# A macaron block on one core: two width tests with branches, TensorE kept busy ahead of the first products, and another order in the opening

## The reference

```python
x = x + 0.5 * ffn(layernorm(x))
x = x + attn(layernorm(x))
x = x + 0.5 * ffn(layernorm(x))
# ffn(x):  h = norm(x) * gamma + beta;  w1 = (fc1_q - 128) * fc1_scales per group of 128 rows
#          y = silu(h @ w1 + fc1_bias);  z = y @ w2 + fc2_bias;  returns x + 0.5 * z
# attn(x): a = sigmoid(x@Wa+ba); b = x@Wb+bb; c = tanh(x@Wc+bc)
#          s = a*s + (1-a)*b over time;  returns (c*s)@Wy + by + x@Wd + bd
```

## Time and profile before

| | |
|---|---|
| median of three runs | 689.95 us |
| the profiled execution | 690.4 us, span 687.6 us, granted clock 0.999 |
| TensorE busy | 668.0 us, 97%, 3224 matmuls |
| ScalarE, VectorE, GpSimd busy | 653.4 (95%), 634.8 (92%), 604.8 us (88%) |
| chain that ended last | TensorE 90%, ScalarE 3%, VectorE 3% |

### The profile page before, as it was taken

One profiled execution on the slowest core, in us unless ns is written; L12 is line 12 of the kernel. 1 busy time (PEld: TensorE's weight loads), 2 busy tenths in 40 slices (PEclk: granted clock), 3 DMA queues, 4 the chain that ended last, 5 costly groups with the idle time before them and its releaser, 6 DMA issues.

```text
span 687.6 us, 13669 instructions
## 1 busy us (share of the span) xinstructions
PE 668.0 (97%) x3224; PEld 539.2 (78%) x3224; DVE 634.8 (92%) x1329; ACT 653.4 (95%) x1095; POOL 604.8 (88%) x673
## 2 busy tenths in 40 slices
PE   3999999999999999999999999999999999999997
PEld 3678888888888878778877887788888888888885
DVE  5789999999999999889999998899999999999987
ACT  4899999999999999889999999999999999999994
POOL 4899999999999999857766789999999999999973
PEclk9999999999999999999999999999999999999999
DMA  8670000000000000000000000000000000000001
GB/s 254 172 236 4 1 0 0 0 0 0 0 0 0 1 0 2 1 1 1 0 0 0 0 1 1 30 33 32 31 31 31 31 31 31 31 31 32 32 32 63
DMA packets 19962, 20.22 MB, mean 29 GB/s; under 512 B 1564, under 2 KB 19666, under 8 KB 19922
## 3 DMA queue, kind: packets, MB, share of 16 engines
q1 hardware_dynamic: 19824, 19.74, 9.3%
q10 hardware_dynamic: 98, 0.02, 0.0%
HBM read 11.37 MB, written 8.39 MB: 29 GB/s over the span
## 4 chain that ended last, share of the span: by engine, by line
PE 90%; ACT 3%; DVE 3%; issue 2%; DMA 1%; ACTq 0%; POOL 0%; DVEq 0%; POOLq 0%
PE ps_z L1009 38%; PE ps_fc L1009 33%; PE ps_fc L1142 8%; PE ps_tr L1002 5%; PE ps_tr L1070 4%; PE ps_fc L1150 2%; PE ps_z L1002 1%; DMA rows<-in_L_attn_bc 1%; DVE z_acc L762 1%; ACT ps_fc L576 1%; ACT g_hi L593 1%; DVE stats L699 1%; ACT g_full L591 0%; DVE resid L887 0%; ACTq L530 0%
## 5 line engine op out<-in xcount | busy, mean ns | idle before, releaser
L410 POOL TENSOR_TENSOR g_lo<-g_full,g_hi 128x512 fp32r<-128x512 f32 x256 | 332.9, 1300 | 24.7 <-ACT g_hi L593 21.8
L762 DVE SCALAR_TENSOR_TENSOR z_acc<-ps_z,cols,z_acc 128x512 f32<-128x512 f32 (+1 forms) x449 | 322.2, 742 | 24.2 <-PE ps_z L1009 16.4
L1009 PE MATMUL ps_fc<-h_hi,q_sb 128*128 128x512 f32 x512 | 213.4, 417 | 1.4 <-ACT ps_fc L576 1.4
L1009 PE MATMUL ps_z<-g_hi,q_sb 128*128 128x512 f32 x512 | 202.4, 395 | 0.1
L1009 PE MATMUL ps_fc<-h_lo,q_sb 128*128 128x512 f32 x512 | 202.3, 395 | 0.0
L1009 PE MATMUL ps_z<-g_lo,q_sb 128*128 128x512 f32 x512 | 200.6, 392 | 0.0
L591 ACT ACTIVATE g_full<-ps_fc,safe_scale 128x512 f32<-128x512 f32 x256 | 194.8, 761 | 3.9 <-PE ps_fc L1009 2.2
L593 ACT ACTIVATE g_hi<-ps_fc,safe_scale 128x512 fp32r<-128x512 f32 x256 | 196.2, 766 | 0.0
L576 ACT ACTIVATE ps_fc<-ps_fc,bias,ratio 128x512 f32<-128x512 f32 x193 | 157.9, 819 | 1.8 <-DVE bias L873 1.8
L1009 PEld LDWEIGHTS ps_z<-g_hi,q_sb 128*128 128x128 f32 x512 | 96.1, 188 | 25.0 <-DVE z_acc L762 2.7
L1009 PEld LDWEIGHTS ps_fc<-h_hi,q_sb 128*128 128x128 f32 x512 | 97.3, 190 | 21.0 <-ACT ps_fc L576 2.1
(11 more groups left out here) (110 smaller groups left out, 820.4 us busy)
## 6 DMA issues: line engine op xcount, KB each, us to landing
resid<-in_L_attn_x SPq DMA_DIRECT2D x15, 512.0 KB, 4.6
out_x<-resid SPq DMA_DIRECT2D x15, 512.0 KB, 2.9
q_int<-in_L_ffn_fc_q SPq DMA_DIRECT2D x4, 512.0 KB, 7.3
resid<-in_L_attn_x SPq DMA_DIRECT2D x2, 256.0 KB, 3.0
out_x<-resid SPq DMA_DIRECT2D x2, 256.0 KB, 2.7
wd_sb<-in_L_attn_Wd SPq DMA_DIRECT2D x1, 256.0 KB
wy_raw<-in_L_attn_Wy SPq DMA_DIRECT2D x2, 64.0 KB
bias_rows<-in_L_attn_by SPq DMA_DIRECT2D x1, 128.0 KB
```

Of the source, the lines that this page charges most:

```text
L410: nc.gpsimd.tensor_tensor(g_lo[:, g % 4, :], g_full[:, g % 4, :], g_hi[:, g % 4, :].bitcast(F32), ALU.subtract).then_inc(g_ready, 1)
L762: nc.vector.scalar_tensor_tensor(out=z, in0=bank_of(g, n, par)[:, tokens], scalar=col(R_S2 + KC * g + n), in1=z, op0=ALU.mult, op1=ALU.add ...
L1009: last = nc.tensor.matmul(out, w, v, start=start and i == 0, stop=stop and i == len(pairs) - 1, skip_group_check=not start)
```

## The change

1. TensorE issues 18 matmuls of 128x512 on a matrix of ones (`keep_busy`) before the rows' transpose, 2 and 3 more around the bias products. Their output is overwritten.
2. The width test is done twice: once for q1 (its two parts joined), once for all. TensorE branches on the first before the opening groups f0 to f3 (`opening`), and on the second before the rest. VectorE has one conditional block as before, now behind the second test, with a nested one for the wide q1 bias.
3. q2's first half is converted on GpSimd, its second on ScalarE. The rows' transpose goes to another bank, and ScalarE copies the columns after its half of xhat and after q1's first chunk. The turns don't wait for the columns.
4. VectorE: ratio, lower_h c0, bias fold and lower_h c1 stand ahead of statistics(1), which stands ahead of the last maximum, the second test and VectorE's half of xhat for tile 1. That half was behind variance(2). `join_largest`, `find_width` and `prepare_wide` take a number for the test and are otherwise what they were.
5. In tile 0: tile 1's rsqrt behind g_low0 and its xhat behind g_low1 on GpSimd, residual at f4 and f5 (was f2 and f3), turns at f5 and f7 (was 3 and 5), lower_h at 6 and 7 (was 4 and 6).

```diff
         halves = (range(0, SUB // 2), range(SUB // 2, SUB))
+        FIRST_TURN_AT, FIRST_LOWER_AT = (5, 7), (6, 7)
+        FIRST_RESIDUAL_AT = {4: (0, 1), 5: (2, 3)}
+        def first_or(ff0, before, first, usual):
+            return first if ff0 == 0 and not before else usual[before]
         q2_halves = (slice(0, FC // 2), slice(FC // 2, FC))
...
                     ff, ln = t + ff0, t + ln0
-                    residual_at, normalise_at = RESIDUAL_AT[before], NORMALISE_AT[before]
+                    residual_at, normalise_at = first_or(ff0, before, FIRST_RESIDUAL_AT, RESIDUAL_AT), NORMALISE_AT[before]
                     for f in range(FC):
...
                             g_low(ff - 1, FC - 1, 1 - par)
-                        elif ff0 == 0:
+                        if ff0 == 0 and not before and f == 1:
                             rsqrt(ln0 + 1, 1, True)
-                        if ff0 == 0 and not before and f == 1:
+                        if ff0 == 0 and not before and f == 2:
                             normalise(ln0 + 1, 1, 1, halves[0], True)
...
                     prepare_columns()
+                    pool.wait_ge(q2_loaded[0], 16)
+                    nc.gpsimd.tensor_scalar(q2_sb[:, q2_halves[0], :], q2_int[:, q2_halves[0], :], -ZERO_POINT, None,
+                                            ALU.add).then_inc(q2_ready[0], 1)
                     residual(ln0, 0, 1)
...
                     convert_q1(0)
+                    act.wait_ge(rows_turned, 1)
+                    nc.scalar.activation(cols[:, :], ps_fc1[:, 3, 0:ROWS], ACT.Copy).then_inc(cols_ready, 1)
+                    act.wait_ge(cols_ready, 1)
+                    convert_q1(1)
                     for c in range(KC):
                         round_h(ln0, ff0, 0, c, bank=(ps_tr, ps_tr2)[c])
-                    convert_q1(1)
-                    for k in range(KC):
-                        act.wait_ge(q2_loaded[k], 16)
-                    nc.scalar.activation(q2_sb[:, :, :], q2_int[:, :, :], ACT.Copy,
-                                         bias=-ZERO_POINT).then_inc(q2_ready, 1)
+                    act.wait_ge(q2_loaded[1], 16)
+                    nc.scalar.activation(q2_sb[:, q2_halves[1], :], q2_int[:, q2_halves[1], :], ACT.Copy,
+                                         bias=-ZERO_POINT).then_inc(q2_ready[1], 1)
                 over_tiles(act, tile)
...
                             add_group(ff if here else ff - 1, (f - LAG) % FC, par if here else 1 - par)
-                        if behind and f in H_LOWER_AT[before]:
-                            lower_h(ln + 1, ff + 1, 1 - par, H_LOWER_AT[before].index(f))
+                        lower_at = first_or(ff0, before, FIRST_LOWER_AT, H_LOWER_AT)
+                        if behind and f in lower_at:
+                            lower_h(ln + 1, ff + 1, 1 - par, lower_at.index(f))
                         if ff0 and not before and f == 0:
...
                             variance(ln0 + 2, 0)
-                            if ff0 == 0:
-                                normalise(ln0 + 1, 1, 1, halves[1])
                         if not before and f == 5:
...
                         largest_of(k, q1_int[:, k, :], q1_loaded[k])
-                    for k, part in enumerate(q2_halves):
-                        largest_of(KC + k, q2_int[:, part, :].rearrange("p g d -> p (g d)"), q2_loaded[k])
-                    join_largest()
+                    join_largest(0, KC)
+                    largest_of(KC, q2_int[:, q2_halves[0], :].rearrange("p g d -> p (g d)"), q2_loaded[0])
+                    find_width(0, KC + 3)
                     dve.wait_ge(scale_done, 3)
                     nc.vector.reciprocal(inverse[:, :], safe_scale[:, :]).then_inc(ratio_ready, 1)
-                    lower_h(ln0, ff0, 0, 0)
-                    find_width()
                     dve.wait_ge(ratio_ready, 1)
                     nc.vector.tensor_tensor(ratio[:, :], cols[:, R_S1:R_S1 + FC], inverse[:, :], ALU.mult)
+                    lower_h(ln0, ff0, 0, 0)
+                    dve.wait_ge(beta_done, KC)
+                    fold_beta(1)
+                    lower_h(ln0, ff0, 0, 1, ps_tr2)
                     dve.wait_ge(x_loaded[1], 16)
...
                     variance(ln0 + 1, 1)
-                    dve.wait_ge(beta_done, KC)
-                    fold_beta(1)
-                    lower_h(ln0, ff0, 0, 1, ps_tr2)
+                    largest_of(KC + 1, q2_int[:, q2_halves[1], :].rearrange("p g d -> p (g d)"), q2_loaded[1])
+                    join_largest(1, 2 * KC + 2)
+                    find_width(1, 2 * KC + 4)
                     prepare_wide()
+                    normalise(ln0 + 1, 1, 1, halves[1])
                 over_tiles(dve, tile)
...
         def _(pe):
+            def keep_busy(count):
+                wide_ones = ones[:, :].rearrange("p (o n) -> p o n", o=1).broadcast_to([P, TILE // P, P])
+                for i in range(count):
+                    nc.tensor.matmul(ps_fc1[:, 1, :].rearrange("p (a n) -> p a n", n=P), ones[:, :], wide_ones,
+                                     start=True, stop=True)
+            pe.wait_ge(ones_ready, 1)
+            keep_busy(18)
             pe.wait_ge(consts_ready, 1)
             pe.wait_ge(rows_loaded, 16 * 9)
-            nc.tensor.transpose(ps_tr2[:, 0:ROWS], rows[:, :], ident[0:ROWS, 0:ROWS]).then_inc(rows_turned, 1)
+            nc.tensor.transpose(ps_fc1[:, 3, 0:ROWS], rows[:, :], ident[0:ROWS, 0:ROWS]).then_inc(rows_turned, 1)
...
                 if n == 0:
-                    if type(ff) is int and ff == 0 and g == 0:
-                        pe.wait_ge(q2_ready, 1)
+                    if type(ff) is int and ff == 0 and g in (0, FC // 2):
+                        pe.wait_ge(q2_ready[g // (FC // 2)], 1)
                     pe.wait_ge(g_ready, FC * ff + (g + 1))
...
                     ff, ln = t + ff0, t + ln0
-                    for f in range(FC):
+                    for f in range(0 if before or ff0 else LAG, FC):
                         half_products(ff, ln, f, par)
...
                             y_products(NT - 1, 1)
-                        if (behind or ff0 == 0) and f in TURN_AT[before]:
-                            c = TURN_AT[before].index(f)
+                        turn_at = first_or(ff0, before, FIRST_TURN_AT, TURN_AT)
+                        if (behind or ff0 == 0) and f in turn_at:
+                            c = turn_at.index(f)
                             if c and before:
...
+            def opening():
+                for f in range(LAG):
+                    half_products(0, 0, f, 0)
+                    if f >= 1:
+                        add_products(0, 0, f - 1, 0)
+            def turn_all_largest():
+                pe.wait_ge(largest_found, 2 * KC + 3)
+                turn_largest(1)
             def program():
...
-            pe.wait_ge(cols_ready, 1)
+            def turn_largest(turn):
+                nc.tensor.transpose(ps_z[0:1, 0, 0:P], largest[:, 4 + turn:5 + turn],
+                                    ident[:, :]).then_inc(largest_turned, 1)
             for c in range(KC):
                 turn(0, 0, c, (ps_tr, ps_tr2)[c], 2, 1)
+            pe.wait_ge(largest_found, KC + 1)
+            turn_largest(0)
+            keep_busy(2)
             pe.wait_ge(beta_ready, 2)
...
             beta_products(0, q1_sb, True).then_inc(beta_done, 1)
-            pe.wait_ge(largest_found, 5)
-            nc.tensor.transpose(ps_z[0:1, 0, 0:P], largest[:, 4:5], ident[:, :]).then_inc(largest_turned, 1)
             pe.wait_ge(q1_ready, KC)
             beta_products(1, q1_sb).then_inc(beta_done, 1)
+            keep_busy(3)
             pe.wait_ge(flag_ready, 1)
-            wide = pe.value_load(wide_flag[0:1, 0:1], min_val=0, max_val=1)
+            q1_wide = pe.value_load(wide_flag[0:1, 0:1], min_val=0, max_val=1)
+            with pe.If(q1_wide < 1):
+                q1_parts = (q1_sb,)
+                opening()
+                turn_all_largest()
+            with pe.Else():
+                q1_parts = (q1_sb, q1_low)
+                turn_all_largest()
+                pe.wait_ge(q1_low_ready, KC)
+                pe.wait_ge(bias_ready, 1)
+                for k in range(KC):
+                    last = beta_products(k, q1_low)
+                last.then_inc(beta_low_done, 1)
+                pe.wait_ge(wide_bias_ready, 1)
+                opening()
+            pe.wait_ge(flag_ready, 2)
+            wide = pe.value_load(wide_flag[0:1, 1:2], min_val=0, max_val=1)
             with pe.If(wide < 1):
...
                 q1_parts, q2_parts = (q1_sb, q1_low), (q2_sb, q2_low)
-                pe.wait_ge(wide_ready, KC + 1)
-                pe.wait_ge(bias_ready, 1)
-                for k in range(KC):
-                    last = beta_products(k, q1_low)
-                last.then_inc(beta_low_done, 1)
-                pe.wait_ge(wide_bias_ready, 1)
+                pe.wait_ge(q1_low_ready, KC)
```

(33 more changed lines are left out.)

39 lines of the change are left out of this document (19 added, 20 removed).

## The result

The changed kernel takes 690.91 us (median of 22 runs, 688.80 to 693.24), the kernel before 689.42 (22 runs, 688.20 to 690.91). The ratio is 1.0023 [1.0015, 1.0032]: slower by 1.5 us. The forecast was 687.0.

The account below looks back on a forecast made before the run. TensorE sets the pace once the loops run, so the opening decides. Its earlier start less the new waits gains 3.0 us: 690.4 - 3.0 = 687.4, or 687.0 against the median 689.95; range 685.2 to 690.2.

Parts of the forecast that it names:

- The new waits: Opening: VectorE waits for rsqrt(1) behind g_low0, so TensorE waits 1.3 us for add f4, later 0.65 before tile 1.
- The sum: Tile 1's fc2(6,0) starts at 34.9 instead of 37.94, a gain of 3.0 us; 4.9 without the two waits.
- the thin stretch: TensorE's sparsely filled time from 9.7 us in the opening, where the clock might not hold.
- rival A: Fillers don't hold the clock in the opening: whole 1.4 us slower, chance 0.11; in part gain 0.5 to 2, 0.13.
- Fillers: TensorE's opening: 18 products end by 9.6, before the rows' transpose, cost nothing; the clock is up from there on.
- ScalarE, TensorE, half f0: Opening of tile 0: half f0 starts at 14.2 instead of 16.94, silu f0 at 16.25 instead of 20.87.
- GpSimd, q2's first half: GpSimd's opening: the conversion takes 2.2 us, 11.7 to 13.9, hidden ahead of g_low0 with 1.4 us to spare.
- Second test: TensorE reads flag 2 and branches on an empty queue: 0.9 us, between 0.4 and 2.5; half f4 at 20.4.
- Rival B: The second branch costs over 2.2 us; at 3.7 us the gain is 1.5, 688.5 us; chance 0.07.
- Tile time behind the opening: Behind the first tiles nothing changes: each tile still takes 16.40 us, TensorE's queue full.
- C: The VectorE and GpSimd waits are shorter than counted: gain to 4.9 us, 685.1; chance 0.09.
- D: The order alone gives nothing, fillers do nothing, ScalarE stays the bound: 689.95 us; chance 0.02.

Follow-up runs that it names:

- c1: The changed kernel with 7 filler products on TensorE ahead of add f4 of tile 0; ratio 1.0015 to the kernel before, 690.49 us.
- d1: The changed kernel with tile 0's g_low as a one-input GpSimd tensor_scalar that writes zeros instead of the subtraction; ratio 0.9973 to the kernel before, 688.17 us.
- d3: Changed kernel with statistics(2) behind scale f4, rsqrt(1) and GpSimd's xhat(1) ahead of g_low0, VectorE's xhat(1) before the skip, statistics(3) at f6; 0.9988, 689.40 us.
- experiment 3: The changed kernel with 14 or 7 filler products on TensorE ahead of add f4 of tile 0; ratios 1.0039 and 1.0015 to the kernel before.
- a4: The changed kernel without its 23 filler products; ratio 1.0045 to the kernel before, 692.5 us.

## Why the prediction was wrong

**The step that failed is *The new waits***: "20.9 + 0.7 + 2.08 + 0.72 = 24.4 [...] and waits 1.3 us". Its mechanism was right but for the last link (add f4 waits for scale f4, scale f4 for statistics(2), that for xhat(1)), its size was not. The last link, xhat(1) waiting for rsqrt(1) behind g_low0, held in none of the nine profiles: in c1 flag 2 was there at 19.07 and xhat(1) began 1.59 us later, at 20.66, with shift there at 20.48. The start was sooner than the forecast's 20.9 even so. But xhat to the start of scale f4 took 4.77 us instead of 2.78: xhat 0.8 more, variance(2) 1.2 more with `neg_mean` alone 1.08. Without its fillers TensorE would have waited from 22.84 to 26.29, 3.45 us. The durations came from rows that begin while GpSimd has nothing to do (xhat, 21.80: GpSimd idle between 20.07 and 22.21), and were moved to a place where it runs g_low.

The end times show it: xhat of after comes in two pieces, 1.22 us to 24.90, just behind g_low's 24.74, and then 0.40; its `neg_mean` ends at 28.49 with g_low's 28.45, and c1's `neg_mean` at 25.51 with a g_low that ends at 25.49. The Trainium skill, "SBUF — State Buffer", section "SBUF: two separate sides", says that VectorE in a 2-port mode and GpSimd share one pair of ports as an exclusive lock, and that whoever comes second stands for the whole instruction. These ends agree, and d1 does in part; d3's xhat, 0.80 us beside a GpSimd tensor_scalar, doesn't fit a lock that always lasts the whole instruction. No run here varies the port mode, so that VectorE stands beside g_low is shown, and that the ports are why is argued.

The kernel before showed it already, in places that the forecast didn't read. Its `var_terms` of a later tile:

```profile
59.99 1.29 POOL L410 TENSOR_TENSOR g_lo<-g_full,g_hi 128x512 fp32r<-128x512 f32 x1 [0.22 <-ACT g_hi L593]
60.82 0.48 DVE L715 TENSOR_SCALAR var_terms<-mean_var 128x4 f32<-128x4 f32 x1
```

They end at 61.28 and 61.30. In that trace 26 of these 128x4 operations start in the middle of a GpSimd tensor_tensor of 128x512, and all 26 last until it ends (0.39 to 0.73 us). A BATCH_NORM_AGGREGATE in the same place isn't held (0.17 us, ended 0.7 before g_low), nor are the two scales of VectorE on TensorE's result (0.80 us, ended 0.3 before it).

**The sum.** The forecast had fc2(6,0) at 34.9; c1 has it at 38.27, 3.4 later. 1.85 of it is add f4 (26.29 for 24.45), and it stands on until tile 1's second turn (32.42), which the forecast put just ahead of tile 1's first product (30.45; 32.80 in c1). The rest, some 1.4, comes from there to fc2(6,0), 5.85 us for 4.45: 0.4 is that turn, the rest a wait for the accumulation, 0.95 in its bracket. `var_terms` stands 1.35 us beside a g_low, and the accumulation behind it is late. The forecast had that stretch as TensorE's own work (34.8), with g_low6 at 34.9. Before had it at 37.94, so with these two terms the gain of 3.0 is a loss of 0.3.

The rest up to 1.5 us isn't split by an experiment. Part of it is the clock that falls in the gap: 0.5 us, from two single profiles (experiment 3); the forecast foresaw a fall only in the thin stretch. And executions differ at the front. The profiled one has x's second half 1.65 us late and its clock at 0.50 from 11 to 14, which is rival A in part: xhat(1) there starts 3.0 us behind c1's (23.68 for 20.66), 1.65 of it by x and 1.36 by the clock. None of the other profiles with this opening has the late x; one, d1, has a half clock near there (from 13.3 to 16.6). The mean granted clock of after's 22 executions lies between 0.991 and 0.999, and the slowest of them have the lowest (692.4 to 693.2 us at 0.991 to 0.993), so how far the clock falls in an execution is part of the loss; how large a part stays open.

**Point by point.**
- *Fillers*: right that they end before the rows (18 in 6.93 us, 1.92 to 8.85). They don't hold the clock in every execution. Worth 1.5 us in after and 1.1 to 1.4 in the kernel before. The way, by single profiles: without them (a4) the 16 bias products take 3.55 us for c1's 1.91, half f0 starts at 14.53 for 13.48 although the rows came sooner, and xhat(1) at 22.95 for 20.66.
- *ScalarE, TensorE, half f0*: forecast 14.2 and silu f0 16.25; c1 has 13.48 and 15.78, sooner than forecast. The profile of after has 16.49 and 18.80: 1.65 for the late x and 1.36 for the half clock.
- *GpSimd, q2's first half*: 2.78 us, not 2.2; hidden, as forecast.
- *Second test*: TensorE's read and branch 0.9 taken, 22.92 - 22.09 = 0.83 measured. Rival B is out (0.91 in c1). VectorE's read and skip, 0.41 taken and hidden behind rsqrt(1), took 1.59 in all nine profiles that show it, and it, not rsqrt(1), set the start of xhat(1).
- *Tile time behind the opening*: 16.40 us, right.
- *Rivals*: C (shorter waits) and D were wrong. The slower side came by none of them alone: a wait of the forecast that was 2.1 us longer than counted, a second one of its kind, and a clock that falls at more places than one.

## What to carry over

A duration read where the neighbour engine is idle is a lower bound where it is not: before moving a small VectorE operation on on-chip data beside GpSimd's large ones, look for a row with both, or charge it the rest of the GpSimd operation. If a trace of the kernel has such pairs, list them before you take a duration from elsewhere. Put the scale that TensorE waits for ahead of everything that only a later tile needs. Reading a flag and skipping a block has a price of its own: look whether it, and not the data, sets the start of the operation behind it. Two edits (statistics(2) behind scale f4, rsqrt(1) ahead of g_low0) turn a loss of 0.23% into a gain of 0.18%.
